# VectorE's order in four places of a fused ViT tower, and one reduction over tiles of one size

## The reference

```python
h = concat([cls, patches @ W_lin.T + b_lin]) + pos                # 32 x 37 x 256

n = layernorm(h)                                                  # attention
K = exp(n @ Wk);  Ks = cumsum(K, tokens) + 1e-6
S = cumsum(K * (n @ Wv), tokens) / Ks
h = h + (S * sigmoid(n @ Wq)) @ Wc

n = layernorm(h)                                                  # feed-forward
u = act_quant(n) @ weight_quant(w1).T                             # 256 -> 1024
u = silu(depthwise_conv1d(u, conv_w, 3 taps, along tokens) + conv_b)
h = h + act_quant(u) @ weight_quant(w2).T                         # 1024 -> 256
```

## Time and profile before

| | |
|---|---|
| profiled execution: its time, and the span of its trace | 173.41 us, 171.6 us |
| busy time in the span | PE 141.1 (82%), DVE 138.3 (81%), ACT 81.7 (48%), POOL 72.2 (42%) |
| granted TensorE clock, mean | 0.93 |
| three timed runs | 172.31, 174.07, 174.29 us |

### The profile page before, as it was taken

How to read it: one execution, slowest core, us unless ns; L and a number is a source line. 1 busy time by engine, 2 the same in 40 slices (tenths; PEclk the granted TensorE clock), 3 DMA queues, 4 the chain that set the end, 5 groups by cost and what they waited for, 6 DMA issues and landing times. The chain is left out here.

```text
span 171.6 us, 2404 instructions
## 1 busy us (share of the span) xinstructions
PE 141.1 (82%) x821; PEld 113.4 (66%) x821; DVE 138.3 (81%) x285; ACT 81.7 (48%) x129; POOL 72.2 (42%) x91
## 2 busy tenths in 40 slices
PE   7878999995797999995999496497499848969961
PEld 5766878784585678983666384496389644957940
DVE  0068555589966668998799999969999999999992
ACT  0625443595532513555771174759338326482120
POOL 5001022485013552083556089764709345109460
PEclk9999999998589999999999999879957985899999
DMA  5999992000000000000000000000200000300013
GB/s 165 286 279 401 348 253 70 0 2 0 4 0 0 2 4 0 0 0 0 0 2 0 4 0 2 0 0 6 65 4 0 0 0 0 83 0 0 2 48 86
DMA packets 4568, 9.08 MB, mean 53 GB/s; under 512 B 910, under 2 KB 3340, under 8 KB 4428
## 3 DMA queue, kind: packets, MB, share of 16 engines
q1 hardware_dynamic: 4256, 8.70, 17.0%
q10 hardware_dynamic: 300, 0.23, 0.7%
HBM read 7.71 MB, written 1.21 MB: 52 GB/s over the span
## 5 line engine op out<-in xcount | busy, mean ns | idle before, releaser
L492 PE MATMUL pair<-linT,xT 128*111 128x256 f32 (+1 forms) x132 | 32.2, 401 | 1.6 <-DVE xT L894 1.6
L492 PEld LDWEIGHTS pair<-linT,xT 128*111 128x111 f32 (+1 forms) x132 | 23.8, 184 | 8.3 <-ACT xT L711 2.1
L403 POOL TENSOR_TENSOR z<-x_flat,s_row 128x666 f32<-128x666 f32 (+1 forms) x12 | 18.1, 1540 | 18.8 <-ACT s_row L787 18.8
L746 ACT ACTIVATE y<-pair,cb_sb,cw_sb 128x333 f32<-128x333 f32 (+2 forms) x32 | 17.2, 597 | 10.6 <-PE pair L538 10.6
L455 PE MATMUL pair<-busy 128*128 128x256 bf16 x147 | 21.2, 301 | 1.2 <-DVE busy L1073 1.2
L455 PEld LDWEIGHTS pair<-busy 128*128 128x128 bf16 x147 | 15.6, 107 | 4.0 <-DVE busy L1073 1.2
L538 PE MATMUL pair<-xq_hi,w1T 128*128 128x334 f32 (+2 forms) x64 | 17.2, 355 | 0.6 <-issue 0.4
L937 DVE RECIPROCAL krec<-ksum 128x333 f32<-128x333 f32 (+2 forms) x8 | 15.8, 1990 | 0.0
L989 DVE SCALAR_TENSOR_TENSOR y<-pair,cw_sb,y 128x324 f32<-128x324 f32 (+2 forms) x32 | 15.0, 510 | 1.0 <-ACT x_flat L757 0.8
L538 PE MATMUL pair<-xq_lo,w1T 128*128 128x334 f32 (+2 forms) x64 | 15.7, 330 | 0.0
L326 POOL TENSOR_TENSOR rstd<-var,minus_half 111x1 f32<-111x1 f32 x6 | 3.4, 574 | 24.6 <-DVE var L1102 24.6
(11 more groups left out here) (124 smaller groups left out, 281.9 us busy)
## 6 DMA issues: line engine op xcount, KB each, us to landing
x_flat<-in_x_dram SPq DMA_DIRECT2D x6, 576.0 KB, 12.4
z<-in_L_ffn_w_dram SPq DMA_DIRECT2D x1, 1024.0 KB, 13.5
y<-in_L_ffn_w_dram SPq DMA_DIRECT2D x1, 1024.0 KB, 16.2
out_dram<-o_sb SPq DMA_DIRECT2D x10, 96.0 KB, 1.7
lin_sb<-in_L_tok_W_lin_dram SPq DMA_DIRECT2D x1, 768.0 KB, 4.8
wk_sb<-in_L_attn_Wk_dram SPq DMA_DIRECT2D x1, 256.0 KB, 10.2
wv_sb<-in_L_attn_Wv_dram SPq DMA_DIRECT2D x1, 256.0 KB, 10.3
wq_sb<-in_L_attn_Wq_dram SPq DMA_DIRECT2D x1, 256.0 KB, 11.1
```

What stands on the lines that cost most here:

```text
L403: nc.gpsimd.tensor_tensor(z_of[f][:, 2 * i:2 * i + 2, :], act_of[f][:, 2 * i:2 * i + 2, :], s_row[:, :T[f]].unsqueeze(1).to_broadcast([P, ...
L492: last = nc.tensor.matmul(ps[:n, j % 2, :D], xT[:, k, FIRST[g] * L + t0:FIRST[g] * L + t0 + n], linT[:, k, :], start=(k == 0), stop=(k == ...
L746: nc.scalar.activation(y(f)[:, k, :], pair(("f1", f, i))[:, b, :T[f]], ACT.Identity, bias=cb_sb[:, k:k + 1], scale=cw_sb[:, k, 1:2]).then_ ...
```

## The change

Four things change; no work is added or dropped.

1. `collect_lo(0)` in turn g = 1 moves from behind the scans to behind `keys_reciprocal(1, 0)` and `embed_add(2, 0)`. In turns 2 and 3 it stays where it was.
2. In turns 0 to 2, `second_moments(g)` moves ahead of `conv_sides(f, 3)`. On POOL, `add_last_tap(f, 3)` moves behind `centre(g)` and the inverse root.
3. In the tail, the rounding of group 1's hidden layer, `quantise_hidden(G - 3)`, moves behind `residual(3)` and `second_moments(3)`.
4. The reductions of `token_scales` and `hidden_scales` are made over all tiles of one size in one instruction: three tiles in groups 1 and 2, two in group 3; in group 0 the two tiles of 111 tokens in one instruction and the one of 74 in another. The reduction in `token_scales` so waits for all its tiles of `cen`.

```diff
+        def equal_tiles(g):
+            full = sum(n == TILES[g][0][1] for _, n in TILES[g])
+            return [(0, full, TILES[g][0][1])] + [(full, NT[g], TILES[g][-1][1])] * (full < NT[g])
...
                 if g < G - 1:                                   # POOL
                     if f >= 0:
-                        for i in BY_POOL:
-                            add_last_tap(f, i)
+                        add_last_tap(f, 1)
                     centre(g)
                     inv_root(var2, rstd2, var2_ok, rstd2_ok, g)
+                    if f >= 0:
+                        add_last_tap(f, 3)
...
-                for j, (t0, n) in enumerate(TILES[g]):          # token_scales
-                    dve.wait_ge(cen_ok, DONE[g] + j + 1)
-                    nc.vector.tensor_reduce(cmax[:n, j:j + 1], cen[:n, j, :], AX.X, ALU.max,
-                                            apply_absolute_value=True).then_inc(cmax_ok, 1)
+                for j0, j1, n in equal_tiles(g):
+                    dve.wait_ge(cen_ok, DONE[g] + j1)
+                    nc.vector.tensor_reduce(cmax[:n, j0:j1], cen[:n, j0:j1, :], AX.X, ALU.max,
+                                            apply_absolute_value=True).then_inc(cmax_ok, j1 - j0)
...
-                for j, (t0, n) in enumerate(TILES[f]):          # hidden_scales
-                    last = nc.vector.tensor_reduce(amax2[:n, j:j + 1], ps[:n, 0, j * wide:(j + 1) * wide], AX.X, ALU.max)
+                for j0, j1, n in equal_tiles(f):
+                    last = nc.vector.tensor_reduce(amax2[:n, j0:j1], ps[:n, 0, j0 * wide:j1 * wide].rearrange(
+                        "p (j c) -> p j c", c=wide), AX.X, ALU.max)
...
-                if f >= 0:                                      # the turn on DVE
+                if e >= 0:
                     collect_lo(f)
                 keys_reciprocal(g, 0)
                 if 0 < g < G - 1:
                     embed_add(g + 1, 0)
+                if g == 1:
+                    collect_lo(f)
...
                     residual(g)
+                    second_moments(g)
                     if f >= 0:
                         conv_sides(f, 3)
-                    second_moments(g)
-
-            quantise_hidden(G - 3)
+
             residual(G - 1)
             second_moments(G - 1)
+            quantise_hidden(G - 3)
             conv_sides(G - 2, 2)
```

## The result

The changed kernel took 170.97, 170.98, 171.08 and 172.58 us (median 171.03); the kernel before, with one more run beside it, a median of 174.18. The ratio is 0.988, 95% interval 0.984 to 0.992: 1.2% faster, 2.0 us, where 172.0 us (1.4 us less than the profiled execution) had been forecast. That is under the 2% which the forecast wanted before it called a change faster, but the interval does not take in 1. Now and then an execution of any of these kernels is 1.5% or more above its fastest, at a lower mean clock; the ratios leave such executions out.

A forecast was written before the change was run, and what follows sets the result against it. The prediction took PE to bound the kernel until 77.4 us and DVE from the middle of turn 2. Gains of 0.18 + 1.01 + 0.18 = 1.37 us off 173.41 gave 172.0 us, range 170.3 to 174.0.

The forecast's parts named there:

- Turn 1: Up to `key_values(2)`: of 3.6 us of DVE gaps only 0.30 us arrive, as V of group 2 on PE releases it.
- Turn 2: Up to `key_values(3)`: 0.18 us gained, the earlier 0.36 included; 0.36 at most, at worst nothing.
- The hold-up by POOL's addition: In `token_scales(2)`: DVE's `step1` waits until POOL's `add_last_tap(1, 3)` ends at 114.7 us; without it 0.18 us better.
- The tail: Between `conv_sides(2, 1)` and `conv_sides(2, 2)`: later rounding shortens 4.80 us to 3.79, gaining 1.01; bounds 1.3 and -0.3.
- The wait of 0.31 us for the attention output: In the tail, ahead of `residual(3)`'s second tile: DVE waits about 0.3 us for PE's output, ending at 133.24 us.
- Merged reductions: In the three `hidden_scales` left: 0.06 us each, 0.18 in all, bounds 0 and 0.15 each; nothing in `token_scales`.
- The sum: Whole kernel: 0.18 + 1.01 + 0.18 = 1.37 us off the profiled execution's 173.41, giving 172.0 us.
- The rival that counts all gaps: Turns 1 and 2: all DVE gaps count, 5.9 us in all, 167.5 us; partly true 169 to 170; chance 0.13.
- The rounding did not stay long: Rival in the tail: POOL's centring comes between the four roundings, no gain there, 173.3 us; chance 0.17.
- The attention output waited: Rival in the tail: slow PE clock delays the output, DVE stands still, 172.0 + 2.5 = 174.5 us; chance 0.08.

The follow-up runs named there:

- parts 1 to 3 together: Kernel before with the three reorderings but all reductions tile by tile: ratio 0.987 (0.982 to 0.993).
- part 2 alone: Kernel before with only `second_moments` ahead of `conv_sides(f, 3)` and POOL's `add_last_tap(f, 3)` behind the inverse root: ratio 0.996 (0.992 to 1.000).
- part 4 alone: Kernel before with only the merged reductions of `token_scales` and `hidden_scales`, in the old order: ratio 1.009 (1.006 to 1.013).
- part 1 alone: Kernel before with only `collect_lo(0)` moved behind a reciprocal and an `embed_add`: ratio 0.998 (0.995 to 1.002).
- part 3 alone: Kernel before with only `quantise_hidden(1)` moved behind `residual(3)` and `second_moments(3)`, run twice: ratios 0.987 and 0.992.

## Why the prediction was right, point by point

1. **Turn 1: right, to the hundredth.** 0.30 us predicted, 0.29 measured, released by PE as written. Part 1 brings none of it, part 2 all. That PE set the end of turn 1 was read from one row, 16.38 busy of 16.40 us. The three traces in which PE's clock fell in turn 1 bear it out: `key_values(2)` came 1.6 us later there, after a wait of 1.9 to 2.3 us for V.
2. **Turn 2: right.** Counted from `key_values(1)`, `key_values(3)` comes at 56.42 us instead of 56.60: 0.18, as predicted, though V of group 3 (ready at 113.49) would have allowed 0.9 us more. The hold-up by POOL's addition is shown: `amax1` ends when it ends, in both turns and also without the merged reductions, and where the addition runs later another small instruction is held. The prediction named `step1` as the one that is held. It was `amax1`, the one that the rule cited beside it adds.
3. **The tail: right in mechanism, and in size partly by luck.** 1.10 us for 1.01. From the first rounding to the step behind the four it is 1.66 us (1.68 predicted), and they kept POOL out of its centring, which the prediction had allowed for: the reduction that needs the centring follows `conv_sides(2, 2)` without a wait, as written. The wait of 0.31 us for the attention output did not come, as PE's clock rose some 4 us earlier; instead `nmean` was held for 0.23 by POOL's last scaling, which runs until 133.00. That one stood in for the other is luck. The same early clock took away the wait of 0.24 us ahead of `conv_sides(2, 0)`. Neither belongs to the change for sure: with parts 1 to 3 together that wait of 0.24 is there again, `nmean` is not held, and the stretch is 3.47 us.

   One thing the prediction did not see: POOL's scaling bounds this place too. In the four traces with the old order the roundings end 1.2 us behind POOL's last scaling, whenever they begin, and take 3.08, 3.25, 3.49 and 3.49 us. What DVE gains ahead of them is lost in them (part 2 alone: 22.03 us from lo to lo, 22.00 before). So in the old order a microsecond saved on DVE was not worth a microsecond here.
4. **Merged reductions: the wrong term.** 0.18 us predicted. 3 x 128 in one instruction takes 0.49 and 0.55 us where three took 0.62 and 0.68, and 2 x 256 takes 0.68 for 0.76: 0.34 in all, more than was worked out. But the last two of these savings do not arrive: from `collect_lo(3)` to `finish_last` it is 22.81 us with `hidden_scales` merged and 22.82 with it tile by tile, at the same wait ahead of `finish_last`. That wait grew by 0.35 with DVE's shorter list, which the prediction did not have, and in `token_scales` the merged reduction costs 0.28 where nothing covers it: part 4 alone made the kernel slower (1.009). In the change the 0.28 is covered by the hold-up. The last two columns together are 43.52 us in the changed kernel, 43.41 with parts 1 to 3 and 43.20 with `hidden_scales` alone merged: a loss of 0.1 to 0.3 instead of a gain of 0.18, and no comparison of times tells it from nothing.
5. **The sum.** 1.37 predicted; 1.51 in the two traces, 2.0 (1.3 to 2.8, from the ratio's interval and 174.07) in the times. That the sum fits so well is luck in part: the 0.35 lost ahead of `finish_last` is about made up by the wait of 0.24 us that went with PE's early clock, and the prediction had neither. Two figures of its range do not add up as written (the bounds give 0.36 + 1.3 + 3 x 0.15 = 2.1 us, not 2.0; 173.41 less 2.0 and 0.8 is 170.6, not 170.3); the measured time lies inside either way. The rival that counts all gaps is excluded by part 1 alone. The rounding did not stay long. The attention output waited in one trace, by 0.55 us and not 2.5.

What carries the change is part 3, whose time alone is clear of no change, together with the 0.3 us of part 2, which only the traces show. That parts 1 and 4 could be left out is also argued from traces; no comparison of times here separates 0.2 us.

## What to carry to other kernels

Before you count a wait that goes away, ask which engine is full in that stretch and which row releases the next step: here the change went for 3.6 us of gaps on VectorE in one turn and brought 0.3, as the waiting moved to other places. A step that moves out from under another engine's long instruction can shrink by more than any gap that the profile lists: the four roundings stood in no list of waits and went from 3.08 us to 1.74. And a merged instruction that has to wait for its last input is worth its saving only where that wait is covered.

## What the runs showed of the hardware

- Instructions of VectorE on 111x3 and 128x12 numbers, 0.16 to 0.18 us otherwise, took 0.73 to 1.52 us and ended within 0.05 us of a GpSimd addition that had begun earlier. The other way round, two GpSimd instructions of 0.93 us together took 2.28 beside four roundings on VectorE. The Trainium skill (SBUF — State Buffer, "Who interferes with whom") has this as an exclusive lock; the rows agree.
- The idle time ahead of the last VectorE step was 0.69 us with 279 or 285 instructions in VectorE's list and 1.04 with 273, the same to 0.02 us in fourteen traces. Cause not found.
- TensorE's clock fell from 1.00 to 0.50 in a wait of 1.80 us ahead of 28 filler matmuls in the two traces with part 3 alone, and stayed at 1.00 through a wait of 1.71 to 1.80 us at the same place in the twelve others. The same 28 matmuls took 4.34 us after the fall and 3.22 without it.
